# The last block of an image in a two-stage convolution kernel: its edge row moved into one small pass, and bias matmuls on summed weights

## The reference

```
off = (sigmoid(conv3x3(x, w_off) + b_off) - 0.5) * 2        # 64 maps: an x and a y shift per channel
sampled = bilinear sample of each channel's own plane at (x - offx, y - offy), reflected at the edge
stage 0:  x = x + conv3x3(sampled, w_dcn) + b_dcn            # 32 -> 32 channels
pooled = mean of gn(x) over the image;  k = (relu(pooled @ w1 + b1)) @ w2 + b2
stage 1:  x = x + depthwise_conv3x3(gn(x), k)                # a 3x3 kernel per image and channel
```

## Time and profile before

| | |
|---|---|
| median of 3 runs | 1601.03 us |
| profiled execution, its own time | 1599.84 us |
| its span from first to last instruction | 1598.0 us |
| PE busy | 1509.8 us (94%), 12048 instructions |
| DVE busy | 1362.4 us (85%) |
| ACT busy | 1054.3 us (66%) |
| POOL busy | 357.6 us (22%) |
| mean granted TensorE clock | 0.985 |
| z, line 357 | 764.3 us, 4608 instructions |
| dc from sr and sh, line 397 | 438.3 and 396.6 us, 4416 instructions |
| dc in the last blocks, lines 401, 404, 406 | 54.4, 32.3 and 32.2 us, 192 each |
| biases, lines 455 and 460 | 7.5 us of 192 and 4.9 us of 384 |

### The profile page before, as it was taken

How to read it: one execution, slowest core, us unless ns; L and a number is a source line. 1 busy time by engine, 2 the same in 40 slices (tenths; PEclk the granted TensorE clock), 3 DMA queues, 4 the chain that set the end, 5 groups by cost and what they waited for, 6 DMA issues and landing times.

```text
span 1598.0 us, 29952 instructions
## 1 busy us (share of the span) xinstructions
PE 1509.8 (94%) x12048; PEld 660.1 (41%) x12048; DVE 1362.4 (85%) x1264; ACT 1054.3 (66%) x1594; POOL 357.6 (22%) x382
## 2 busy tenths in 40 slices
PE   3778888999999999999999999999999999999888
PEld 1333334444444444444444444444444444444343
DVE  3999999999998998989989998899999999899800
ACT  4667566675777667775677757876687765655423
POOL 3000421205031230405121051302404041410010
PEclk9899999999999999999999999999999999999999
DMA  7365454765767567675667757676576665656446
GB/s 247 109 193 154 125 162 151 218 193 173 234 192 251 177 190 238 200 229 159 220 203 224 219 156 241 193 235 189 179 250 202 210 189 161 199 163 199 121 129 226
DMA packets 225274, 307.78 MB, mean 193 GB/s; under 512 B 16656, under 2 KB 167552, under 8 KB 225136
## 3 DMA queue, kind: packets, MB, share of 16 engines
q1 hardware_dynamic: 223632, 304.42, 61.8%
q0 software_dynamic: 1504, 1.45, 0.3%
HBM read 190.18 MB, written 38.14 MB: 143 GB/s over the span
## 4 chain that ended last, share of the span: by engine, by line
PE 65%; DVE 17%; ACT 7%; DMA 5%; issue 4%; SPq 2%; POOL 0%; DVEq 0%; ACTq 0%; POOLq 0%
PE z L357 31%; PE dc L397 16%; PE dw L427 12%; DMA st<-in_planes 3%; DVE nb L720 3%; DVE nb L717 3%; DVE nb L722 3%; PE dc L427 2%; DVE xv L710 2%; DVE nb L724 2%; DVE nb L726 2%; DVE nb L711 1%; DVE yr L743 1%; PE dc L401 1%; ACT dv L536 1%
## 5 line engine op out<-in xcount | busy, mean ns | idle before, releaser
L357 PE MATMUL z<-xv,wos 128*64 128x384 f32 x4608 | 764.3, 487 | 10.7 <-ACT du L536 10.7
L357 PEld LDWEIGHTS z<-xv,wos 128*64 128x64 f32 x4608 | 333.4, 136 | 424.6 <-issue 416.3
L397 PE MATMUL dc<-sr,wds 128*32 128x384 f32 x2304 | 438.3, 522 | 36.2 <-DVE yr L743 36.2
L397 PE MATMUL dc<-sh,wds 128*32 128x384 f32 x2112 | 396.6, 523 | 0.0
L703 DVE COPY_PREDICATED nb<-mu,xv 128x2280 f32<-128x2280 uint16 x96 | 271.2, 2825 | 32.8 <-ACT mu L543 32.4
L427 PE MATMUL dw<-yr,wy 128*64 128x388 f32 x672 | 250.7, 494 | 7.1 <-ACT ot L571 7.1
L427 PE MATMUL dw<-yh,wy 128*64 128x388 f32 x672 | 250.9, 494 | 0.0
L397 PEld LDWEIGHTS dc<-sr,wds 128*32 128x32 f32 x2304 | 134.0, 111 | 274.1 <-issue 273.9
L557 ACT ACTIVATE nb<-xv 128x2292 f32<-128x2292 f32 x96 | 203.0, 2114 | 0.4 <-DVE sr L731 0.4
L536 ACT ACTIVATE du<-z,ob 128x768 f32<-128x768 f32 x96 | 86.1, 897 | 154.9 <-PE z L357 151.3
L710 DVE COPY_PREDICATED xv<-mv,xv 128x768 f32<-128x768 uint16 x96 | 103.1, 1074 | 83.1 <-ACT mv L543 62.8
(11 more groups left out here) (118 smaller groups left out, 1615.7 us busy)
## 6 DMA issues: line engine op xcount, KB each, us to landing
xv<-in_x SPq DMA_DIRECT2D x272, 384.0 KB, 4.7
yr<-in_xr SPq DMA_DIRECT2D x96, 392.0 KB, 7.0
out<-ot SPq DMA_DIRECT2D x96, 388.0 KB, 5.4
yh<-yr SPq DMA_DIRECT2D x179, 196.0 KB, 5.0
st<-in_planes SPq DMA_DIRECT2D x56, 576.0 KB, 7.1
sh<-sr SPq DMA_DIRECT2D x160, 194.0 KB, 2.8
sh<-sr SPq DMA_DIRECT2D x32, 145.5 KB, 2.5
yr<-in_planes SPq DMA_DIRECT2D x8, 576.0 KB, 9.9
```

The source lines that it names most:

```text
L357: last = nc.tensor.matmul(acc[m], weights[:, kx, :], view[:, :, kx:kx + W], start=kx == 0, stop=kx == 2)
L397: last = nc.tensor.matmul(dc[m, q, 0:NB * PAIRS], weights[:, kx, q], view[:, :, cols], start=first, stop=final)
```

## The change

The last block's `dc` is now computed as every other block's, with the ordinary weights and one matmul of 384 columns (line 414 of the new kernel). Its last group of rows then holds one wrong row contribution for each of the two output rows, and lacks one. A new pass of six matmuls of 96 columns per q adds what corrects this ("exchange"): its input `fe` has, in four strips of partitions, the mean row, two real rows and the mean row, and its weights `wde` have positive signs for what is to be added and negative for what is to be taken away. `wde` is one host-made tensor `wdc` times `rxs`, the deviation's reciprocal with a sign per partition. The two real rows and the wrapped row are brought by DMAs: one more where a block is the first of an image, two more where it is the last, and the DMA that went to a spare row of `sh` goes to `se` now and is copied from there (lines 300 to 317).

For the biases the three column taps of the unscaled weights are summed once at the start (`wo_sum`, `wd_sum`, four POOL instructions), and the mean is scaled instead (`mr`), so 12 matmuls stand where 36 stood. PE waits for `mr` in place of the scaled weights. One more constant is loaded at the start.

```diff
 def s_dmas(n):
-    return 2 + (n % CHUNKS % SS == 0)
+    return 2 + (n % CHUNKS % SS == 0) + 2 * (n % CHUNKS == CHUNKS - 1)
...
                 if j == 0:
-                    sp.dma_start(sh[hi, SS * NB + b % 2, :], sr[lo, k, :]).then_inc(done, 16)
+                    sp.dma_start(se[hi, b % 2, :], sr[lo, k, :]).then_inc(se_in[b % 2], 16)
+                    sp.dma_start(fe[2 * C:3 * C, b % 2, :], sr[0:C, k, :]).then_inc(done, 16)
                     sp.dma_start(sh[hi, k:k + NB - 1, :], sr[lo, k + 1:k + NB, :]).then_inc(done, 16)
...
+                if j == CHUNKS - 1:
+                    sp.wait_ge(se_in[b % 2], 16 * (b // 2 + 1))
+                    sp.dma_start(sh[hi, k + NB - 1, :], se[hi, b % 2, :]).then_inc(done, 16)
+                    sp.dma_start(fe[C:2 * C, b % 2, :], sr[P - C:P, k + NB - 1, :]).then_inc(done, 16)
...
-                            if r == 0 or j < CHUNKS - 1:
-                                last = nc.tensor.matmul(dc[m, q, 0:NB * PAIRS], weights[:, kx, q], view[:, :, cols],
-                                                        start=first, stop=final)
-                                continue
-                            n3 = (NB - 1) * PAIRS
-                            nc.tensor.matmul(dc[m, q, 0:n3], weights[:, kx, q], view[:, 0:NB - 1, cols],
-                                             start=first, stop=False)
-
-                            nc.tensor.matmul(dc[m, q, n3:n3 + PAIRS], wde[:, 0, kx, q], view[:, NB - 1, cols],
-                                             start=False, stop=False)
-                            last = nc.tensor.matmul(dc[m, q, n3:n3 + PAIRS], wde[:, 1, kx, q],
-                                                    sh[:, SS * NB + b % 2, cols], start=False, stop=final)
+                            final = final and (r == 0 or j < CHUNKS - 1)
+                            last = nc.tensor.matmul(dc[m, q, 0:NB * PAIRS], weights[:, kx, q], view[:, :, cols],
+                                                    start=first, stop=final)
+                if j == CHUNKS - 1:
+
+
+                    n3 = (NB - 1) * PAIRS
+                    for kx in range(3):
+                        for h in range(2):
+                            m = slice(C * (2 + h), C * (2 + h) + C)
+                            last = nc.tensor.matmul(dc[m, q, n3:n3 + PAIRS], wde[:, kx, q],
+                                                    fe[:, b % 2, kx + h:kx + h + W - 1:2], start=False, stop=kx == 2)
...
-                pe.wait_ge(wo_ok, b + 1)
-                pe.wait_ge(wd_ok, b + 1)
+                pe.wait_ge(mr_ok, 2 * b + 1)
                 small_turn("ob", b)
-                mean = nmx[b % 2][:]
+                mean = mr[b % 2][:]
                 for i in range(2):
-                    for kx in range(3):
-                        for m in halves:
-                            nc.tensor.matmul(sm[m, C_OB + i:C_OB + i + 1], wos[b % 2][:, i, kx], mean,
-                                             start=kx == 0, stop=kx == 2)
+                    for m in halves:
+                        nc.tensor.matmul(sm[m, C_OB + i:C_OB + i + 1], wo_sum[:, i], mean, start=True, stop=True)
...
+                tt(mr[b % 2][:], nmx[b % 2][:], rx[:], ALU.mult).then_inc(mr_ok, 1)
+                tt(rxs[:], kc[:, K_SIGN], rx[:], ALU.mult).then_inc(mr_ok, 1)
...
-            def set_first_edge(b):
-                q = slice(0, P // 2)
-                ts(sh[q, SS * NB + b % 2, :], zero[q, 0:WP], mx[b % 2][q], None, ALU.add).then_inc(h_pads, 1)
+            def set_edges(b):
+                if b >= 2:
+                    pool.wait_ge(dcn_mm, Q * CHUNKS * (b - 1))
+                pool.wait_ge(pads, pads_set(CHUNKS * b + 2))
+                for at, q in enumerate((slice(0, C), slice(P - C, P))):
+                    ts(fe[q, b % 2, :], zero[q, 0:WP], mx[b % 2][q], None, ALU.add).then_inc(h_pads, 1)
+                    pool.wait_ge(h_pads, 2 * b + at + 1)
...
             pool.wait_ge(loaded, LOADED)
+            tt(wo_sum[:], wo[:, :, 0], wo[:, :, 1], ALU.add).then_inc(w_sums, 1)
+            tt(wd_sum[:], wd[:, 0], wd[:, 1], ALU.add).then_inc(w_sums, 1)
+            pool.wait_ge(w_sums, 2)
+            tt(wo_sum[:], wo_sum[:], wo[:, :, 2], ALU.add).then_inc(w_sums, 1)
+            tt(wd_sum[:], wd_sum[:], wd[:, 2], ALU.add).then_inc(w_sums, 1)
+            pool.wait_ge(w_sums, 4)
```

More of the change, by code:

```diff
@@ L51 @@
 K_AVG, K_EYE, K_CEN = slice(0, P), slice(P, P + CQ), slice(P + CQ, P + CQ + TAPS)
+K_SIGN = slice(P + CQ + TAPS, P + CQ + TAPS + 1)
+K_ALL = P + CQ + TAPS + 1
 M_LOC, V_LOC, M_REL, V_SQ, M_SQ, DEV, DEV_SQ, V_ALL, V_EPS, D_STD = (
@@ L58 @@
 BANDS = [(g, o) for o in range(2) for g in range(G) if 0 <= g - o <= 2]
-LOADED = 16 * 9
+LOADED = 16 * 10
 X_STEPS, Y_STEPS = 9, 10
@@ L126, in block_kernel @@
         sr = sb("sr", [P, SS * NB, WP])
-        sh = sb("sh", [P, SS * NB + 2, WP])
+        sh = sb("sh", [P, SS * NB, WP])
         yr = sb("yr", [P, YS * NB, Q, PW])
@@ L135, in block_kernel @@
         wo = sb("wo", [P, 2, 3, 2 * C])
+        wo_sum = sb("wo_sum", [P, 2, 2 * C])
+        wd_sum = sb("wd_sum", [P, Q, C])
+        mr = [sb(f"mr{s}", [P, 1]) for s in range(2)]
         wos = [sb(f"wos{s}", [P, 2, 3, 2 * C]) for s in range(2)]
@@ L138, in block_kernel @@
         wds = [sb(f"wds{s}", [P, 3, Q, C]) for s in range(2)]
-        wde = sb("wde", [P, 2, 3, Q, C])
+        wdc = sb("wdc", [P, 3, Q, C])
+        wde = sb("wde", [P, 3, Q, C])
+        rxs = sb("rxs", [P, 1])
+        se = sb("se", [P, 2, WP])
+        fe = sb("fe", [P, 2, WP])
         wy = [sb(f"wy{s}", [P, Q, 2, 2 * C]) for s in range(2)]
@@ L146, in block_kernel @@
         bd = sb("bd", [P, Q])
-        kc = sb("kc", [P, P + CQ + TAPS])
+        kc = sb("kc", [P, K_ALL])
         zero = sb("zero", [P, 2 * WP])
@@ L186, in block_kernel @@
         s_sh = [sem(f"s_sh{s}") for s in range(SS)]
+        se_in = [sem(f"se_in{s}") for s in range(2)]
         y_sh = [sem(f"y_sh{s}") for s in range(HS)]
@@ L221, in block_kernel @@
         we_ok = sem("we_ok")
+        w_sums = sem("w_sums")
+        mr_ok = sem("mr_ok")
         wy_ok = sem("wy_ok")
@@ L385, in deform @@
                         pe.wait_ge(h_pads, 2 * b + 2)
-                        pe.wait_ge(we_ok, 2 * b + 2)
+                        pe.wait_ge(we_ok, b + 1)
                 wait(pe, y_done, Q * (n - 1) + q + 1)
@@ L447, in x_biases @@
             def x_biases(b):
-                pe.wait_ge(wo_ok, b + 1)
-                pe.wait_ge(wd_ok, b + 1)
+                pe.wait_ge(mr_ok, 2 * b + 1)
                 small_turn("ob", b)
-                mean = nmx[b % 2][:]
+                mean = mr[b % 2][:]
                 for i in range(2):
-                    for kx in range(3):
-                        for m in halves:
-                            nc.tensor.matmul(sm[m, C_OB + i:C_OB + i + 1], wos[b % 2][:, i, kx], mean,
-                                             start=kx == 0, stop=kx == 2)
+                    for m in halves:
+                        nc.tensor.matmul(sm[m, C_OB + i:C_OB + i + 1], wo_sum[:, i], mean, start=True, stop=True)
                 for q in range(Q):
[L458 to L461, removed]
+                    for g in range(G):
+                        last = nc.tensor.matmul(sm[C * g:C * g + C, C_DB + q:C_DB + q + 1], wd_sum[:, q], mean,
+                                                start=True, stop=True)
                 last.then_inc(small, 1)
@@ L746, in evacuate @@
                         accum_out=ys1[b % 2][:, q, j:j + 1]).then_inc(y_done, 1)
-            dve.wait_ge(cleared, 4)
+            dve.wait_ge(cleared, 3)
             dve.wait_ge(piv, 1)
@@ L810, in edge_weights @@
                 wait(pool, dcn_mm, Q * CHUNKS * b)
[L811 to L815, removed]
+                pool.wait_ge(mr_ok, 2 * b + 2)
+                ts(wde[:], wdc[:], rxs[:], None, ALU.mult).then_inc(we_ok, 1)
+                pool.wait_ge(we_ok, b + 1)
             def set_pads(n):
@@ L932, in _ @@
                     set_pads(i + 2)
-                if 0 < b <= B and o == 0:
-                    set_last_edge(b - 1)
                 if b < B and o == 0:
-                    set_first_edge(b)
+                    set_edges(b)
                 if b < B and o < SS:
@@ L978 @@
     order = np.arange(C).reshape(CQ, Q).T.reshape(C)
-    consts = np.zeros((P, P + CQ + TAPS), np.float32)
+    consts = np.zeros((P, K_ALL), np.float32)
+    consts[:, K_SIGN] = np.where((p // C == 0) | (p // C == G - 1), 1, -1)[:, None]
     consts[:, K_AVG] = (pc[:, None] == pc[None, :]) / (2.0 * G)
@@ L1002 @@
     w_dcn = bands(asc(L0_conv_w_dcn)[order][:, order].transpose(2, 1, 3, 0))
+    w_edge = np.zeros((G, C, 3, Q, 2, CQ), np.float32)
+    by_row = w_dcn.reshape(G, C, 3, 2, Q, CQ)
+    w_edge[2, ..., 0, :] = w_edge[3, ..., 0, :] = by_row[2, ..., 0, :, :]
+    w_edge[1, ..., 1, :] = w_edge[0, ..., 1, :] = by_row[1, ..., 1, :, :]
```

(1 more changed line is left out.)

14 lines of the change are left out of this document (3 added, 11 removed).

## The result

| | before | changed |
|---|---|---|
| median of the runs on one chip, us | 1600.92 (4 runs, 1599.07 to 1601.81) | 1589.97 (4 runs, 1588.77 to 1592.29) |
| ratio, 95% interval | | 0.9941 (0.9927 to 0.9954) |
| profiled execution, us | 1599.84 | 1589.68 |
| its span, us | 1598.0 | 1587.9 |
| mean granted clock | 0.985 | 0.986 |

The forecast was 1588.5 us, the median is 1589.97. The changed kernel is 0.6% faster by the recorded ratio; the quotient of the two medians is 0.9932, within its interval. The profiled execution is 10.2 us shorter where 12.5 were forecast. Each kernel has one profiled execution, so differences of a microsecond or two between single stretches of two profiles are weak evidence.

The account below looks back on a forecast made before the run. PE was taken as the bound from the third image, with a DVE and ACT loop close behind. The loop allows 11.8 us, 13.5 with the tail, less 1.0 for SP: 12.5 off, 1588.5 us as median, range 1584 to 1595.5.

Parts of the forecast that it names:

- The last block: PE's last block of an image: the split's 2.79 us go, the new pass adds 1.1, saving 1.7 us per image.
- The serial rival: The pass's two strips run one after the other, 2.2 us, last block saves only 0.6: 1592.5 us, chance 0.13.
- The biases: PE's bias matmuls fall from 1.30 to 0.43 us, saving 0.87 us per image, possibly only 0.6.
- PE in all: PE's savings after the second image: six last blocks and five sets of biases, 14.6 us, plus 1.7 in the tail.
- What the other cycle allows: From block 24 to 95 the DVE and ACT loop lets at most 11.8 of PE's 14.6 us be had.
- The loop: DVE's sampling to ACT's sum of squares to mask `mv` and back to DVE: 183.3 us per image.
- the one on SP: SP's added DMA issues make `st` later: 0 to 1.65 us per image, taken as 0.15 six times, 1.0 in all.
- the first images: In the first two images DVE and ACT set the pace, so no saving was counted.
- Tail: At the end DVE waits 9.5 us for the last block's matmuls; the 1.7 us saved there come off in full.
- The start: A tenth load and four POOL sums before the normalisation: 0 together, bounds 0.5 us faster and 1 slower.
- What was to show it: Signs in the profile after; forecast wrong if middle images stay above 184.5 us or fall under 183.
- The slower rival: PE's new waits at the start of `dc` lower its clock, 1.54 us per fall: 1607 us, chance 0.04.

Follow-up runs that it names:

- before_st_first: The kernel before, with the load of ACT's tile `st` issued at the start of SP's step: 1595.44 us, ratio 0.9975.
- st_first: The changed kernel with the load of ACT's tile `st` issued at the start of SP's step: 1581.07 us, ratio 0.9880.
- sp_late: The changed kernel with its three added DMAs per image issued at the end of SP's step, behind the loads: 1589.63 us, ratio 0.9931.
- combo: `combo2` with the three added DMAs also issued at the end of SP's step: 1568.73 us, ratio 0.9804.
- square_late: The changed kernel with ACT's sum of squares issued behind both masks of the step: 1573.50 us, ratio 0.9838.
- bias_only: The kernel before with only the bias change (summed taps, 12 matmuls in place of 36): 1595.35 us, ratio 0.9969.
- edge_only: The changed kernel with the old biases, so the kernel before with only the new last block: 1594.95 us, ratio 0.9964.
- combo2: The changed kernel with `st` loaded first, the sum of squares behind the masks and the start's four sums moved into POOL's waits: 1566.63 us, ratio 0.9800.
- st_first_no_pass: `st_first` without the last block's pass of short matmuls, so edge rows are not corrected: 1579.40 us, ratio 0.9879.
- combo2_no_pass: `combo2` without the last block's pass of short matmuls, so edge rows are not corrected: 1558.19 us, ratio 0.9736.

## Why the prediction was right

**The last block: right.** 5.35 us measured, 5.4 forecast, the pass 1.1. The serial rival (1592.5) is out: at 24 x 0.09 the two passes would have cost 2.2. It had been read out of "TensorE: Matmul & The Clock Gate", Part 3 of the Trainium skill: matmuls start and end strictly in program order. For the starts this trace doesn't agree: the first matmuls of q = 1 start at 985.11 and the second half of the pass, which stands ahead of them in the program, at 985.18, on other strips. The inference was also too strong. Even with starts strictly in order, the second instruction of one matmul and the first of the next, on the other strip, could start together, which gives seven starts 0.09 apart for the 12 instructions, an estimate of 0.63 us and not 1.1. So the 0.62 alone would not have decided between the two readings; the order of the starts does.

**The biases: 0.74 and not 0.87.** The term counted 0.43 for what is left; 0.56 was measured. A part does not shrink with the count: from the last start of the 64-column kind to the first of the 32-column kind are 0.13 us in both kernels, and from the last of these to `dw` 0.10. The prediction had a fixed part ("filling and draining") as its other end, a saving of 0.6; the saving lies between.

**PE in all: right.** 1.73 + 0.74 = 2.5 us per image, against 1.7 + 0.87 forecast. With the tile early in both kernels, four images took 9.9 us less (741.9 in `before_st_first`, 732.0 in `st_first`), 2.5 each. PE's saving arrives in full there.

**What the other cycle allows: the mis-sized term.** The sum capped the blocks 24 to 95 at 1096.3 - 11.8 = 1084.5 and put 1.0 on top for SP. DVE's sample ends of blocks 12, 24 and 95 (answers to the earlier trace rows):

```profile
228.90 0.96 DVE L744 TENSOR_TENSOR sr<-nb 128x768 f32<-128x768 f32 x1
...
411.70 0.96 DVE L744 TENSOR_TENSOR sr<-nb 128x768 f32<-128x768 f32 x1
...
1501.32 0.96 DVE L744 TENSOR_TENSOR sr<-nb 128x768 f32<-128x768 f32 x1
```

| | forecast | measured |
|---|---|---|
| up to block 24 | 0 | -2.2 (414.87 to 412.66) |
| block 24 to 95 | -11.8 + 1.0 | -6.7 (1096.3 to 1089.6) |
| block 95 to the end | -1.7 | -1.2 (86.8 to 85.6) |
| sum | -12.5 | -10.1 |

The loop itself was sized well (183.05 for 183.3). But the image took 183.8 to 184.8 and not 183.3: 4.1 us more than forecast from block 24 to 95. The term that was mis-sized is the one on SP. It priced only the *added* issues, at 1.0 (their place is worth nothing measurable, as `sp_late` and `combo` show). The tile's lateness in the kernel before stood in its own rows, with a wait of 0.35 on DVE, and it counted nothing for that: `st_first` shows 8.9 us in all, 5.3 of them in images 4 to 7. The lateness had been hidden by PE (`before_st_first`: 0.4 in the same images). In the changed kernel the loop, 183.05, and PE, 182.99, are equally long. That the loss needs both the late tile and the loop is shown (`st_first` and `square_late` each remove it); that the pipeline then has no time left to make up for a step that ACT begins late is my reading of the waits, and not shown by itself.

**Counted at nothing: the first images, -2.2.** The first image is 3.0 us shorter (179.1 to 176.1), of which the later start of `z` (29.16 to 29.81) takes 0.65 back before block 12 is sampled; at block 24 2.2 are left. But `bias_only` has 414.38 there, `sp_late`, which differs from the changed kernel only in the place of three DMAs, 414.58, and `edge_only` 416.12, against 414.87 before. So the -2.2 may be the scatter of single executions. It offset half of the miss in the profiled execution, and that part of the agreement is luck.

**Tail: -1.2 for -1.7.** DVE's wait for the last block's matmuls fell by 1.7, as forecast (the earlier trace rows has 9.5), from 1480 us on:

```profile
DVE yr L756 <- PE dc L423: 7.8, 2, 5.9
```

**The start: 0.65 later,** inside its bounds of -0.5 to +1, but not for the reason given. The four sums took POOL until 21.25, and the normalisation began at 21.75, not 20.71, after a wait of 0.50 on ACT. ACT waited for DVE's sums of the first tiles, and DVE for its loads: the sixth landed at 16.47, not 15.50. `edge_only`, without any sum on POOL, began at 21.92, and `combo2`, with the sums after it, at 21.42. So the sums on POOL did not set this start; why the loads land later is open.

**What was to show it.** Last block 5.4 (5.35), biases 0.43 (0.56), small PE waits at a clock of 1.00, ACT's wait for `st` 1.1 longer (the longest is 5.2 for 4.1): there. That PE's waits would be on `yr` before `dc` was wrong: they are on `ot` before `dw`. That isn't due to the tile alone, for in `st_first_no_pass`, where no tile is late and the loop binds, they are on `ot` too. DVE's image was to be near 183.5; images 4 to 7 are 184.1, 183.8, 184.8 and 184.6, and two of the four exceed the 184.5 above which the forecast was to count as wrong, though their mean, 184.3, doesn't. So by the prediction's own sign the cap by the loop is not the whole account, though the total came out; the late tile is the rest. The slower rival, a fall of the clock, did not occur: with 6.1 us of waits in 15 pieces the granted clock stayed at 1.00.

## What to carry to other kernels

When two cycles lie within 1% of each other, a faster first one is worth what the second allows *with every small delay that the first used to cover*: list the in-order queues in which an instruction waits on a DMA, and count what stands behind it, before pricing only what is new. The new wait often shows on another instruction than the cycle suggests, so test with a cure on each side. Here one load per step issued earlier (some 16 us in the step shown) gave 9 us, and ACT's sum of squares put behind the masks 16.5, beside 11 from the change itself. And where a cure leaves the wait in place, as `square_late` does with `mv`, look at what the releaser itself waits for.

## What the runs showed of the hardware

POOL beside DVE. The four sums at the start, in the changed kernel while DVE sums its first tiles with two inputs, and then two of them in `combo2`, where DVE has finished these:

```profile
16.35 0.45 POOL L930 TENSOR_TENSOR wo_sum<-wo 128x128 f32<-128x128 f32 x1 [9.03 <-DMA wdc<-in_w_edge]
16.77 1.43 POOL L931 TENSOR_TENSOR wd_sum<-wd 128x64 f32<-128x64 f32 x1
18.27 1.58 POOL L933 TENSOR_TENSOR wo_sum<-wo_sum,wo 128x128 f32<-128x128 f32 x1
19.82 1.43 POOL L934 TENSOR_TENSOR wd_sum<-wd_sum,wd 128x64 f32<-128x64 f32 x1
```

```profile
21.97 0.45 POOL L931 TENSOR_TENSOR wo_sum<-wo 128x128 f32<-128x128 f32 x1
22.39 0.31 POOL L932 TENSOR_TENSOR wd_sum<-wd 128x64 f32<-128x64 f32 x1
```

The same sum of 64 columns takes 0.31 us alone (22.39) and 1.43 beside DVE (16.77), about the length of one of DVE's instructions (1.42). "SBUF — State Buffer" of the Trainium skill (section "Who interferes with whom") says that a DVE instruction with two inputs contends with a POOL instruction that reads; the trace agrees.

Short matmuls on two strips. The instructions of 96-column float32 matmuls come at 0.052 us each on two strips where one strip needs 0.09, and those of q = 0 run among 384-column matmuls of other strips (984.92 to 985.18). The pass's 24 instructions cost 1.1 us among long ones (`combo2` against `combo2_no_pass`).
